# Attention scores made transposed on two column halves of the array and turned back, in an attention and feed-forward block on one core

## What is computed

```python
Q = (q @ Wq.T).reshape(b, s, HKV, exp, DK)
K = (k @ Wk.T).reshape(b, s, HKV, DK)
V = (v @ Wv.T).reshape(b, s, HKV, DV)
scores = jnp.einsum('bqhed,bkhd->bheqk', Q, K) * scale
scores = jnp.where(causal, scores, jnp.finfo(scores.dtype).min)
probs = jax.nn.softmax(scores, axis=-1)
attn = jnp.einsum('bheqk,bkhd->bqhed', probs, V)
attn = attn.reshape(b, s, H * DV)
return attn @ Wd.T
...
x = x + jnp.tanh(g_xattn[0]) * attention(_layernorm(x), ctx)
x = x + jnp.tanh(g_ffn[0]) * ffn(_layernorm(x))
```

## Time and profile before

| | |
|---|---|
| median of 3 runs | 1547.43 us (1546.60 to 1548.42) |
| the profiled execution, its own time | 1546.4 us |
| its span, first to last instruction | 1544.6 us |
| TensorE matmuls busy | 1514.7 us, 98% |
| VectorE | 1104.0 us, 71% |
| ScalarE | 564.3 us, 37% |
| GpSimd | 731.2 us, 47% |
| mean granted TensorE clock | 0.995 of full |

### The profile page before, as it was taken

How to read it: one execution, slowest core, us unless ns; L and a number is a source line. 1 busy time by engine, 2 the same in 40 slices (tenths; PEclk the granted TensorE clock), 3 DMA queues, 4 the chain that set the end, 5 groups by cost and what they waited for, 6 DMA issues and landing times.

```text
span 1544.6 us, 21445 instructions
## 1 busy us (share of the span) xinstructions
PE 1514.7 (98%) x7842; PEld 1265.9 (82%) x7842; DVE 1104.0 (71%) x1672; ACT 564.3 (37%) x976; POOL 731.2 (47%) x636
## 2 busy tenths in 40 slices
PE   7999999999999999999999999999999999999998
PEld 7898978778888888888888888888877787888886
DVE  4155578988778776776777787777587687767676
ACT  3123335444444333333333333333344334333332
POOL 0122279998788121121112232234376776766663
PEclk9999999999999999999999999999999999999999
DMA  6446557767987543333333333342011111311212
GB/s 233 137 156 224 184 188 268 239 235 254 356 311 254 194 144 112 128 112 134 130 109 113 127 110 109 117 143 79 21 42 56 47 42 55 103 62 41 62 55 69
DMA packets 114808, 214.40 MB, mean 139 GB/s; under 512 B 9616, under 2 KB 47760, under 8 KB 112656
## 3 DMA queue, kind: packets, MB, share of 16 engines
q1 hardware_dynamic: 114704, 213.03, 41.4%
HBM read 147.46 MB, written 65.54 MB: 138 GB/s over the span
## 4 chain that ended last, share of the span: by engine, by line
PE 89%; DVE 6%; issue 3%; DMA 1%; ACT 1%; POOL 0%; POOLq 0%; SPq 0%; DVEq 0%; ACTq 0%
PE bank L440 66%; PE bank L558 7%; PE bank L589 4%; PE bank L699 3%; PE bank L700 3%; PE bank L701 3%; PE bank L574 2%; DVE el L1034 1%; DVE X L1195 1%; DVE er L1034 1%; PE bank L498 1%; DMA k_scratch<-k_st 1%; PE bank L613 0%; PE bank L488 0%; DVE bn L990 0%
## 5 line engine op out<-in xcount | busy, mean ns | idle before, releaser
L1339 POOL TENSOR_TENSOR wd_lo<-wd_raw,wd_hi 128x512 fp32r<-128x512 f32 x64 | 93.1, 1476 | 385.0 <-ACT wd_hi L815 385.0
L440 PE MATMUL bank<-wd_hi,o_hi 128*128 128x512 f32 x512 | 207.0, 404 | 0.0
L440 PE MATMUL bank<-wd_hi,o_lo 128*128 128x512 f32 x512 | 200.0, 391 | 0.0
L440 PE MATMUL bank<-wd_lo,o_hi 128*128 128x512 f32 x512 | 199.6, 390 | 0.0
L440 PE MATMUL bank<-xc_hi,wa_hi 128*128 128x512 f32 x448 | 176.1, 393 | 3.0 <-DVE t L1065 1.2
L440 PE MATMUL bank<-xc_hi,wa_lo 128*128 128x512 f32 x448 | 174.6, 390 | 0.0
L440 PE MATMUL bank<-xc_lo,wa_hi 128*128 128x512 f32 x448 | 174.5, 390 | 0.0
L440 PE MATMUL bank<-x_hi,wf_hi 128*128 128x512 f32 x392 | 155.1, 396 | 10.3 <-issue 9.1
L1195 DVE SCALAR_TENSOR_TENSOR X<-bank,tg,X 128x512 f32<-128x512 f32 x224 | 156.7, 742 | 0.2 <-PE bank L701 0.2
L440 PE MATMUL bank<-x_hi,wf_lo 128*128 128x512 f32 x392 | 154.0, 393 | 0.0
L440 PE MATMUL bank<-x_lo,wf_hi 128*128 128x512 f32 x364 | 143.1, 393 | 0.0
(11 more groups left out here) (145 smaller groups left out, 3557.0 us busy)
## 6 DMA issues: line engine op xcount, KB each, us to landing
q_scratch<-q_st SPq DMA_DIRECT2D x32, 1024.0 KB, 4.4
q_sb<-q_scratch SPq DMA_DIRECT2D x64, 512.0 KB, 3.5
wq_raw<-in_wq SPq DMA_DIRECT2D x32, 512.0 KB, 4.3
wd_raw<-in_wd SPq DMA_DIRECT2D x16, 1024.0 KB, 4.8
f_raw<-ffn_eff_scratch SPq DMA_DIRECT2D x28, 512.0 KB, 3.7
er_raw<-in_sf_r SPq DMA_DIRECT2D x42, 256.0 KB, 2.9
e_raw<-in_wf SPq DMA_DIRECT2D x42, 256.0 KB, 5.0
ffn_eff_scratch<-e_eff SPq DMA_DIRECT2D x42, 256.0 KB, 4.8
```

The lines of the kernel that those rows point to most:

```text
L440: last = pe.matmul(to, a, b, start=(start and n == 0), stop=(stop and n == 3 * len(pairs) - 1), skip_group_check=onto)
L1339: g.tensor_tensor(wd_lo[h % 2][:, e, :], wd_raw[:, e, :], f32(wd_hi[h % 2][:, e, :]), ALU.subtract).then_inc(g_wd, 1)
```

## The change

scores(u) now takes k_sb as the stationary operand (64 columns: the keys of one sequence) and q_sb as the moving one (256 columns: 4 query heads by 64 tokens). It makes 4 matmuls. The result has keys on the partitions: sequence b = 0 of a pair on partitions 0 to 63, b = 1 on 64 to 127. A new semaphore p_st tells of it. ScalarE copies bank 6 to a new SBUF tile st (scores_out, semaphore a_st), and score_transposes turns it back into bank 6 by four 128x128 transposes, after which p_s is raised as before. The DMA of q_sb and k_sb waits for p_st in place of p_s.

The order of the loop changes. Before, an iteration i was: first half of the output of unit i-2, probability transposes of i-1, scores of i, weighted values of i-1, second half of the output of i-2. Now it is: scores of i, weighted values of i-1, score transposes of i, both halves of the output of i-2, probability transposes of i. VectorE adds both halves to X after the softmax of unit i. At the end, the weighted values of the last unit come between the two halves of the output of unit 62. In the last quads the score transposes stand behind the first product, and weighted_values(0) behind them.

```diff
@@ tiles, semaphores
+    st = [at(143, "st0", [P, 512]), at(203, "st1", [P, 512])]
...
+    p_st, p_s, p_pt, p_o, p_y = sem("p_st"), sem("p_s"), sem("p_pt"), sem("p_o"), sem("p_y")
+    a_st = sem("a_st")
@@ load_q_k
-                sp.wait_ge(p_s, u - 1)
+                sp.wait_ge(p_st, u - 1)
@@ TensorE, quad
             product(q, 1, 0, 0, 0)
+            if q >= NQ - 2:
+                score_transposes(q - NQ + 2)
+            if q == NQ - 1:
+                weighted_values(0)
@@ TensorE, scores
-            for cb in range(CB):
-                for ep in range(2):
-                    n = 4 * (cb // 2) + 2 * ep + cb % 2
-                    last = pe.matmul(bank[6][:, n * S:(n + 1) * S],
-                                     q_sb[u % 2][:, ep, cb, :, :].rearrange("p e s -> p (e s)"),
-                                     k_sb[u % 2][:, cb * S:(cb + 1) * S], start=True, stop=True)
+            for t in range(CT):
+                for b in range(2):
+                    cb = 2 * t + b
+                    last = pe.matmul(bank[6][b * S:(b + 1) * S, t * 256:(t + 1) * 256],
+                                     k_sb[u % 2][:, cb * S:(cb + 1) * S],
+                                     q_sb[u % 2][:, :, cb, :, :].rearrange("p a e s -> p a (e s)"),
+                                     start=True, stop=True)
+            last.then_inc(p_st, 1)
+
+        def score_transposes(u):
+            pe.wait_ge(a_st, u + 1)
+            for n in range(4):
+                last = pe.transpose(bank[6][:, n * P:(n + 1) * P], st[u >= 2][:, n * P:(n + 1) * P], ident[:, :])
             last.then_inc(p_s, 1)
@@ TensorE, the loop
-                weighted_values(0)
             quad(q)
-        for i in range(2, NU + 1):
+        prob_transposes(1)
+        for i in range(2, NU):
+            scores(i)
+            weighted_values(i - 1)
+            score_transposes(i)
             output(i - 2, 0)
-            prob_transposes(i - 1)
-            if i < NU:
-                scores(i)
             if i in COLUMNS1:
...
-            if i < NU:
-                weighted_values(i - 1)
             output(i - 2, 1)
+            prob_transposes(i)
+        output(NU - 2, 0)
         weighted_values(NU - 1)
+        output(NU - 2, 1)
@@ ScalarE, quad
             if q == NQ - 1:
                 probs_out(0)
-                out_hi(0)
-            elif q:
+            if q >= NQ - 2:
+                scores_out(q - NQ + 2)
+            if 0 < q < NQ - 1:
                 left_hi(q + 1)
...
+            if q == NQ - 1:
+                out_hi(0)
@@ ScalarE, new, and its loop
+        def scores_out(u):
+            a.wait_ge(p_st, u + 1)
+            if u == 0:
+
+                a.wait_ge(g_wa, 3 * (NQ - 1))
+            if u:
+                a.wait_ge(p_s, u)
+            a.activation(st[u >= 2][:, :], bank[6][:, :], ACT.Copy).then_inc(a_st, 1)
...
             probs_out(i - 1)
+            if i < NU:
+                scores_out(i)
             out_hi(i - 1)
@@ VectorE, quad and the loop
+            if q == NQ - 1:
+                out_lo(0)
...
-            add_to_x(i - 2, 0)
             if i < NU:
                 masked_minus_max(i)
-            if i < NU:
                 out_lo(i - 1)
                 normalised(i)
+            add_to_x(i - 2, 0)
             add_to_x(i - 2, 1)
```

More of the change, by code:

```diff
@@ L169, in flamingo @@
     p_p = {n: sem(f"p_p{n}") for n in range(1, 8)}
-    p_s, p_pt, p_o, p_y = sem("p_s"), sem("p_pt"), sem("p_o"), sem("p_y")
+    p_st, p_s, p_pt, p_o, p_y = sem("p_st"), sem("p_s"), sem("p_pt"), sem("p_o"), sem("p_y")
     p_f = {n: sem(f"p_f{n}") for n in range(1, 8)}
@@ L1226, in _ @@
         for q in range(NQ):
-            if q == NQ - 2:
-                masked_minus_max(0)
-            if q == NQ - 1:
-                masked_minus_max(1)
-                out_lo(0)
+            if q >= NQ - 2:
+                masked_minus_max(q - NQ + 2)
             quad(q)
```

## The result

The changed kernel takes 1532.97 us (median of four runs, 1530.42 to 1534.63) beside 1547.08 for the kernel before. The ratio is 0.9906, 95% interval 0.9889 to 0.9923. The forecast was 1534.4, and the sign, the range and the size hold. The sum behind it does not hold in every term: two errors of some 5 and 3 us stand against each other, so that the forecast came this close is partly luck.

The account below looks back on a forecast made before the run. TensorE's instruction order and number were taken to bound the attention stage; -20.2 - 0.3 + 3.9 + 1.6 + 1.0 + 1.0 = -13.0 on 1546.4 gave 1533.4, or 1534.4 against the median, with an 8-in-10 range of 1520 to 1560 us.

Parts of the forecast that it names:

- Part 1: Scores of each unit: transposed, with column halves side by side, they cost 0.86 us for 1.79, a gain of 0.93.
- Rival (a): Scores of every unit: column halves run one after the other, 0.86 us each, +55 us, 1590 us; chance 0.12.
- Rival (b): Scores: halves run side by side but weight loads are exposed, +0.22 to +0.44 us a unit, 1548 to 1562; chance 0.12.
- Part 2: Turning scores back in each unit: four more transposes, 0.43 us, plus a third change of array shape, 0.175.
- Rival (d): Each unit: third shape change free and 64-column loads halve the exposed ones, -0.2 to -0.25 us, 1520 us; chance 0.06.
- Part 3: ScalarE's copy of the scores to SBUF: hidden behind TensorE's work by 0.2 us, cost 0.
- Part 4: New order, VectorE's softmax chain: 0.09 us early, but late beside GpSimd; stalls of 3.9 and 1.6 us, X additions 1 us.
- The two very long multiplies: VectorE's multiply in two units takes 1.69 us; stalls of 0.8 each, 1.6 us, were forecast.
- Row statistics and x_lo: VectorE work following the additions to X: about 0.3 us shows in 3 or 4 units after long multiplies, 1 us.
- Rival (c): VectorE's chain binds in every unit, stalls of 0.15 to 0.25 us, +9 to +15 us, 1544 to 1550; chance 0.12.
- Part 5: End of the loop: the first feed-forward product waits barely for the last addition to X, +1.0 us.
- Half clock: Feed-forward stage: starting 13 us earlier, it may meet none or four of the half-clock stretches, +-3 us.

Follow-up runs that it names:

- the one-half experiment: Against the changed kernel: from the second unit on, all score matmuls write to partitions 0 to 63, so the second sequence's scores are not computed; 1587.14 us.
- The start experiment: Against the changed kernel: last e_eff store issued ahead of the last queries' store, second wd_raw load issued three quads earlier; 1528.23 us.

## Why the prediction was right, and where it was not

**Part 1, the scores: right.** For the time from scores to weighted values 0.86 + 0.175 was forecast and 1.014 measured, and the one-half experiment at 1.87 puts the rest of the doubt away. Rival (a) is refuted: it is what the one-half kernel does, at 1587 us. Rival (b) is refuted too: with exposed loads the step would be 1.25 or more. The Trainium skill (TensorE: Matmul & The Clock Gate, Part 3, The mechanism) has weight loads overlap running matmuls only when the row groups differ, and in the same section also when the load goes to a background weight buffer. Here all score matmuls use all rows, their eight loads lie beside running matmuls (885.59 to 886.22), and the block reaches the next stage in 1.014 us, change of shape included. The trace does not agree with the first form taken alone; whether it is the second is not shown. One reading of the prediction is off without effect: two streams of 256 columns in 0.215 us are 6% faster than 512 in 0.228, not "no faster".

**Part 2, turning back: right.** At full pace a unit needs 0.434 + 0.86 + 0.86 + 0.434 + 5.47 = 8.06. It lasts 8.58, so 0.52 remains for three changes of shape, 0.17 each in the mean; 0.175 was used. The Trainium skill's rule that a change of tiling mode drains TensorE (TensorEngine Tiling, Key Properties) agrees as far as the price goes: 0.52 for three changes where two took 0.35, so the third is paid like the others. Rival (d) needed it free and did not come.

**Part 3, the copy: right.** It ends 0.34 us before it is needed. The prediction said 0.2, but its own terms for TensorE's side, 0.215 + 0.175 + 0.86 + 0.175, make 1.42 and not 1.3, which leaves 0.35.

**Part 4, the chain: right in kind, too dear by some 5 us.** Forecast for 62 units: -20.2 + 3.9 + 1.6 + 1.0 = -13.7. Measured: -18.7. Four terms make the difference. The short units gained 0.335 and not 0.325 (0.6 in all). The long ones lost 0.085 each and not 0.15, as the chain's slack is 0.27 where the sum had 0.09 + 0.12 = 0.21 (1.7 in all). The two very long multiplies do not occur: the longest one of this kernel takes 1.05 (1.6). Before, GpSimd came late from other work and began a tile at 906.34, 0.15 ahead of the multiply at 906.49, which then waited for nearly all of it; now such a late tile begins at 893.35, behind the multiply that starts at 892.61 and takes 0.69. Row statistics and x_lo cost nothing visible: one unit of 8.88 has its 0.3 back in the next, 8.36 (1.0). The step that went wrong was to add a duration read in one order (1.04, or 1.69) to a start in another. The experiments with longer chains show that such a duration is a waiting time: the multiply ends 0.54 after the tile that it met, whenever it began. The Trainium skill (GPSIMD Engine Reference, Key points) says that GpSimd shares its SBUF interfaces with VectorE and contends with instructions that have two SBUF inputs. The multiply is one, and the trace agrees; it shows beyond that that the multiply waits for the whole tile. Rival (c), the chain late everywhere, is refuted by short units that stay the same with 0.23 more on it.

**Part 5, the end: right.** 1.0 forecast, 1.1 in the trace, 1.2 back when undone.

**What was missed: the start, some 3.4 us.** The sum priced the first two units at -0.3 and moved no DMA. The change put o_lo earlier in VectorE's order. Its second buffer shares a place with e_eff, whose store stands in SP's queue behind another store. The prediction worked out a unit in the steady loop, and did not look at the first turn of the loop, where the tiles of the stage before still hold their places. The start experiment returned 2.5 of it; the 0.8 ahead of the first probability transposes was not tried.

**Half clock.** Forecast as +-3 us for the feed-forward stage; it was 1.6 there. That it can also come behind the new waits at the loop's start was not foreseen. The four runs of the changed kernel lie in two pairs, 1530.4 and 1531.7 at a mean clock of 0.997, 1534.3 and 1534.6 at 0.994, and the median falls between them. The forecast of 1534.4 met 1533.0 by luck as far as -5.0 and +3.4 nearly cancel. The profiled execution closes the sum: -13.0 forecast, -5.0, +3.4, +1.7 of the feed-forward stage and -3.2 of the earlier stages make -16.1, for a span 16.0 shorter.

## What to carry to other kernels

When a matmul uses only half of the array's columns and another independent one stands next to it, give them different column halves: here two fp32 matmuls of 64 columns then cost what one does, and that paid for turning the result back. Read a long duration on an engine that shares SBUF with another as a wait with a fixed end, and price it by where that end falls in the new order; if the other engine has time, let it start behind. And when an order is moved, walk through its first and last turn by themselves, with every tile that shares its place with the stage before and every transfer that stands ahead in the queue.

## What the runs showed of the hardware

- Score matmuls of the two column halves overlap whether they alternate in the queue or stand in blocks of two: 1.014 and 1.021 us for the four, and 1.87 us when all four use one half.
- A change of the array's shape costs 0.17 us in the mean of three in a unit. Read from the starts in the unit at 885, over the usual steps and with the longer first step behind it, it is 0.15 from the full array to column halves (0.202 for 0.109, then 0.267 for 0.215), 0.21 from these to row halves (0.316 and 0.320 for 0.215) and 0.16 from row halves to the full array (0.313 for 0.215, then 0.168 for 0.109).
- VectorE's multiply of two SBUF tiles ends 0.54 to 0.55 us after the GpSimd tile that it met: 0.69 alone, 0.81, 1.04 and 1.80 beside one. GpSimd's pair of tiles takes 2.98 when the multiply runs between them and 2.50 to 2.53 when it does not.
- Waits of TensorE of nearly the same length at the start of the loop were followed by a stretch at a granted clock of 0.50 in some executions (2.05 and 2.22 us from start to start) and by full clock in others (2.05 and 2.32). With the same instructions up to there, the start took 51.4 us in one case and 48.6 in the other.
